# Two forms of an FFN change places, and three weight loads go through DRAM scratch

## What is computed

```python
x = x + attn(layernorm(x))        # time mixing, WKV recurrence, W_o
x = x + ffn(layernorm(x))

def ffn(x):                        # every linear: einsum('bsi,oi->bso', x, w) * s
    h = silu(lin(x, w1)) * lin(x, w2)      # 256 -> 1024
    h = gelu(lin(h, h1))                   # 1024 -> 1024
    h = gelu(lin(h, h2))                   # 1024 -> 1024
    return lin(h, w3)                      # 1024 -> 256
```

## Time and profile before

| | us |
|---|---|
| median of 3 runs | 1565.36 |
| lowest, highest | 1562.19, 1566.46 |
| profiled execution | 1566.22 |
| its span, first to last instruction | 1564.5 |
| PE busy in the span | 1496.0 (96%) |
| DVE busy | 1229.2 (79%) |
| ACT busy | 1091.7 (70%) |

### The profile page before, as it was taken

How to read it: one execution, slowest core, us unless ns; L and a number is a source line. 1 busy time by engine, 2 the same in 40 slices (tenths; PEclk the granted TensorE clock), 3 DMA queues, 4 the chain that set the end, 5 groups by cost and what they waited for, 6 DMA issues and landing times.

```text
span 1564.5 us, 28750 instructions
## 1 busy us (share of the span) xinstructions
PE 1496.0 (96%) x10226; PEld 1329.3 (85%) x10226; DVE 1229.2 (79%) x1595; ACT 1091.7 (70%) x1617; POOL 282.5 (18%) x515
## 2 busy tenths in 40 slices
PE   8489999999999999999999999999999999999997
PEld 5269889898888979889897988989888897988897
DVE  7869696987868788686887968788786878868663
ACT  5848676685867768585776867668585776868564
POOL 0201203112030311204021120311213031120300
PEclk9789999999999999999999999999999999999999
DMA  9957466374655737466474746737465573746654
GB/s 365 350 176 240 124 196 213 105 237 123 205 168 164 239 93 243 108 210 190 131 234 104 232 130 195 214 114 232 127 207 158 161 240 94 242 109 206 181 187 110
DMA packets 95893, 287.78 MB, mean 184 GB/s; under 512 B 9216, under 2 KB 33920, under 8 KB 94848
## 3 DMA queue, kind: packets, MB, share of 16 engines
q1 hardware_dynamic: 87168, 279.11, 54.8%
q0 software_dynamic: 8704, 8.39, 4.5%
HBM read 262.30 MB, written 31.46 MB: 188 GB/s over the span
## 4 chain that ended last, share of the span: by engine, by line
PE 50%; issue 17%; ACT 13%; POOL 10%; DVE 4%; POOLq 1%; ACTq 0%; DVEq 0%
PE acc L540 13%; PE acc L542 12%; PE acc L514 7%; PE acc L515 7%; PE att L466 7%; ACT op_hi L746 3%; ACT blocks L786 3%; POOL fresh L1541 2%; POOL norm L1539 2%; ACT norm L673 2%; POOL newton L1522 1%; PE acc L571 1%; POOL newton L1524 1%; DVE parts L1236 1%; ACT L712 1%
## 5 line engine op out<-in xcount | busy, mean ns | idle before, releaser
L540 PE MATMUL acc<-op_hi,ring 128*128 128x256 f32 x3584 | 865.0, 286 | 1.4 <-DVE parts L1236 1.4
L542 PE MATMUL acc<-op_lo,ring 128*128 128x256 f32 x3584 | 841.5, 278 | 0.0
L540 PEld LDWEIGHTS acc<-op_hi,ring 128*128 128x128 f32 x3584 | 674.1, 188 | 21.0 <-issue 19.9
L542 PEld LDWEIGHTS acc<-op_lo,ring 128*128 128x128 f32 x3584 | 673.3, 188 | 11.9 <-issue 10.8
L1193 DVE TENSOR_TENSOR op_lo<-blocks,op_hi 128x1024 fp32r<-128x1024 f32 (+1 forms) x272 | 343.8, 1283 | 68.0 <-ACT op_hi L746 65.9
L746 ACT ACTIVATE op_hi<-blocks 128x1024 fp32r<-128x1024 f32 (+1 forms) x272 | 297.1, 1104 | 83.8 <-DVE blocks L1188 81.2
L1538 POOL TENSOR_TENSOR v_sb<-mix_v,v_sb 128x1024 f32<-128x1024 f32 (+1 forms) x17 | 39.0, 2293 | 867.7 <-DVE r_sb L1145 867.7
L514 PE MATMUL acc<-x_hi,w_rnd 128*128 128x512 f32 x448 | 180.7, 403 | 5.7 <-issue 5.7
L515 PE MATMUL acc<-x_lo,w_rnd 128*128 128x512 f32 x448 | 178.4, 398 | 0.0
L786 ACT ACTIVATE blocks<-parts,vec 128x256 f32<-128x256 f32 x256 | 109.2, 497 | 60.9 <-DVE parts L1231 52.6
L786 ACT ACTIVATE blocks<-acc,vec 128x256 f32<-128x256 f32 x256 | 100.6, 476 | 66.7 <-PE acc L542 66.7
(11 more groups left out here) (135 smaller groups left out, 1943.9 us busy)
## 6 DMA issues: line engine op xcount, KB each, us to landing
ring<-scratch SPq DMA_DIRECT2D x448, 512.0 KB, 4.2
x_in<-in_x SPq DMA_DIRECT2D x32, 256.0 KB, 4.7
stage<-in_w_ffn SPq DMA_DIRECT2D x4, 2048.0 KB, 22.3
scratch<-stage SPq DMA_DIRECT2D x8, 1024.0 KB, 19.5
out<-x_next SPq DMA_DIRECT2D x32, 256.0 KB, 5.0
out<-mix_v POOLq DMA_DIRECT2D x32, 256.0 KB, 4.5
scratch<-in_w_ffn SPq DMA_DIRECT2D x6, 1024.0 KB, 33.1
w_raw<-in_w_ffn SPq DMA_DIRECT2D x3, 1024.0 KB, 11.6
```

The lines of the kernel that those rows point to most:

```text
L540: pe.matmul(out, act(w), act(op_hi[:, k, c, :]), start=(begins and c == 0 and m % 2 == 0), stop=False, skip_group_check=True)
L542: mm = pe.matmul(out, act(w), act(op_lo[:, k, c, :]), start=False, stop=(c == QC - 1), skip_group_check=True)
```

## The change

PE's `If` takes `flag == 0` with the exact form as its body, and the general form moves to the `Else`. PE's wait for the sums' stores goes (SP keeps its own). `w_rnd` is a tile of its own and `w_raw` a view of it as float32. W1, W2, W3 are copied from the input to a new DRAM tensor `w_plain`, and loaded from there into the tile; the three copies stand ahead of the H loads, the three loads behind them, each after a wait of SP. The three roundings with their flag loads and branches go from ACT, DVE and POOL, as do PE's waits for them. ACT's checks of W1 and W2 move from among the copies of tile 0 to behind the checks of H1's blocks.

```diff
-        w_raw = overlay("w_raw", [P, NW], F32)
         w_rnd = sb("w_rnd", [P, NW], F32R)
+        w_raw = w_rnd[:].bitcast(F32)
...
+        w_plain = nc.dram_tensor("w_plain", [3, P, W12], F32, kind="Internal").ap()
...
-            sp.dma_start(w_raw[:, W1_AT:W1_AT + W12], w_ffn[:, 0:W12]).then_inc(ld_w1, 16)
-            sp.dma_start(w_raw[:, W2_AT:W2_AT + W12], w_ffn[:, W12:2 * W12]).then_inc(ld_w2, 16)
+            for n, a in enumerate((0, W12, 2 * W12 + 2 * HH)):
+                sp.dma_start(w_plain[n], w_ffn[:, a:a + W12]).then_inc(st_w[n], 16)
             for l in range(2):
                 for half in range(2):
                     a = 2 * W12 + l * HH + half * 2 * Q
                     sp.dma_start((stage1, stage2)[l][:, 2 * Q * half:2 * Q * (half + 1)], w_ffn[:, a:a + 2 * Q]).then_inc(ld_h[l][half], 16)
-            sp.dma_start(w_raw[:, W3_AT:W3_AT + W3], w_ffn[:, 2 * W12 + 2 * HH:]).then_inc(ld_w3, 16)
+            for n, (a, loaded) in enumerate(((W1_AT, ld_w1), (W2_AT, ld_w2), (W3_AT, ld_w3))):
+                sp.wait_ge(st_w[n], 16)
+                sp.dma_start(w_raw[:, a:a + W12], w_plain[n]).then_inc(loaded, 16)
...
-                    if exact:
-                        pe.wait_ge(rounded_w1, 1)
-                        pe.wait_ge(rounded_w2, 1)
...
-                    if exact:
-                        pe.wait_ge(rounded_w3, 1)
...
-            for l in range(2):
-                pe.wait_ge(st_sums[l], 16 * 4)
             flag = pe.value_load(general[0:1, 0:1], min_val=0, max_val=1)
-            with pe.If(flag > 0):
+            with pe.If(flag == 0):
+                mlp(exact=True)
+            with pe.Else():
                 mlp(exact=False)
-            with pe.Else():
-                mlp(exact=True)
...
-            check_piece(w_raw[:, W1_AT:W1_AT + W12], (ld_w1, 16))
             for n, s in enumerate(FIRST):
                 copy_kvr(s, 0, range(DC))
-            check_piece(w_raw[:, W2_AT:W2_AT + W12], (ld_w2, 16))
...
             check_blocks(0)
+            check_piece(w_raw[:, W1_AT:W1_AT + W12], (ld_w1, 16))
+            check_piece(w_raw[:, W2_AT:W2_AT + W12], (ld_w2, 16))
             check_sums(0)
...
-            act.wait_ge(flag_set, 1)
-            flag = act.value_load(general[0:1, 0:1], min_val=0, max_val=1)
-            with act.If(flag == 0):
-                rounded(act_copy_, W2_AT, W12).then_inc(rounded_w2, 1)
...
-            dve.wait_ge(flag_set, 1)
-            flag = dve.value_load(general[0:1, 0:1], min_val=0, max_val=1)
-            with dve.If(flag == 0):
-                rounded(dve.tensor_copy, W1_AT, W12).then_inc(rounded_w1, 1)
...
-            pool.wait_ge(flag_set, 1)
-            flag = pool.value_load(general[0:1, 0:1], min_val=0, max_val=1)
-            with pool.If(flag == 0):
-                rounded(pool.tensor_copy, W3_AT, W3).then_inc(rounded_w3, 1)
```

More of the change, by code:

```diff
@@ L284, in build @@
         flag_max = ctx.enter_context(nc.semaphore("flag_max"))
-        rounded_w1, rounded_w2, rounded_w3 = (ctx.enter_context(nc.semaphore(n)) for n in ("rounded_w1", "rounded_w2", "rounded_w3"))
+        st_w = [ctx.enter_context(nc.semaphore(f"st_w{n + 1}")) for n in range(3)]
         W1_AT, W2_AT, W3_AT = 0, W12, 2 * W12
@@ L295, in build @@
         S3_ = [RAW[0][A21_], RAW[1][A21_]]
-        def rounded(copy, a, n):
-            return copy(w_rnd[:, a:a + n], w_raw[:, a:a + n])
         first_chains = Chain(ctx, nc, "first_dve_chain"), Chain(ctx, nc, "first_pool_chain")
@@ L848, in _ @@
             act.wait_ge(setup_pool, 2)
-            def act_copy_(dst, src):
-                return act.activation(dst, src, ACT.Copy)
             checked = [0]
```

## The result

The changed kernel takes 1567.9 us (median of 20 runs, 1565.12 to 1570.53) against 1565.32 for the kernel before beside it (20 runs, 1562.18 to 1568.16): a ratio of 1.0018, with a 95% interval of 1.0012 to 1.0024. It is 2.6 us slower, inside the 0.3% that the prediction called "the same". The profiled run is low among its own: 1565.33 us, with a span of 1563.6.

The account below looks back on a forecast made before the run. It took PE's first FFN matmul (83.82 us) to bound what changes: cheap branch gives 79.3, later checks add 5.5, so 84.8, +1.0 us; median forecast 1566.3 us, range 1562.0 to 1571.0.

Parts of the forecast that it names:

- the gate: Start of PE's first FFN matmul in the first pass, at 83.82 us before, predicted at 84.8.
- The branch: PE's jump to the exact form ahead of the gate: 4.565 us becomes 0.05 by falling through, 4.5 off the gate.
- Binds nothing now: PE's wait for the sums' stores ahead of the flag's load: no effect before, though it would bind at 85.
- the corner: At the gate: flag's load starting before 77.9 without the sums' wait, 78.2 instead of 79.3, at most 1.1 us.
- The end's jump: PE's exact form jumps over the general one at program end: 0.05 to 4.6 us, hidden in 7.7, price 0.
- the end shows: Rival at program end: PE's taken jump costs over 7.7 us and becomes visible, 1567 to 1569 us; chance 0.02.
- The roundings: ACT loses 1.90 us at 74.76, x2 ready 1.8 earlier, but filler and branch hold PE: worth 0.
- The checks: W1's and W2's checks join ACT's row without gaps: 4.2 us, 5.5 later with waiting for the loads.
- The way through DRAM: Three extra weight copies, 9.3 us more DMA: W1 back at 43.3, W2 at 45.7, last sums near 85.
- The rival of copies slower than 340 GB/s: Copies into w_plain run slower and shift all behind: at 4 us a piece gate 87.6, 1569.1 us; chance 0.07.
- x for the next tile: First pass: x_in, queued behind the sums, lands about 87.3 to 88.5; 88.9 still free; price 0.
- from there to ln1 are 6.6 us: First pass: from DVE starting on x_in to ACT's ln1, through POOL's last step, takes 6.6 us.

Follow-up runs that it names:

- swap alone: Kernel before with one edit: PE's If takes flag == 0 with the exact form as its body, general form in the Else; 1560.86 us, ratio 0.9974.
- without the wait: Kernel before with PE's two forms exchanged and PE's waits for the sums' stores removed; 1562.15 us, ratio 0.9981.
- with x early: Kernel before with forms exchanged, PE's wait for the sums' stores gone, next tile's x loaded ahead of those stores; 1561.47 us, ratio 0.9975.
- swap and checks: Kernel before with forms exchanged and ACT's checks of W1 and W2 moved behind those of H1's blocks, weights straight from the input; 1565.8 us, ratio 1.0000.
- x early: Changed kernel with next tile's x loaded ahead of the sums' stores, DVE waiting for these before its first product; 1564.36 us, 0.9997 against the kernel before.

## Why the prediction came out as it did

**Result.** Forecast +1.0 us (1566.3, range 1562.0 to 1571.0) and "the same" at 0.81; it came to +2.6, the same by that bound, and slower beyond the measurement's error. The structure held: a gain and a loss of nearly one size. Several terms were mis-sized, and that the sum came this near is partly luck: the errors went both ways. By the traces the gate is 0.75 us later (83.4 for 82.7, means of three), the second pass 0.9, and the end adds 0.6.

**The branch.** Predicted 4.5 off the gate, measured 4.0 alone. The mechanism was right (0.095 us where it falls through), the term was too large by some 0.7, as one trace gave 4.565 and three give a mean of 3.87. The gate of that first trace was late for this reason, and because its wait for the sums ended later. The branch's length may go with the traffic: 3.37, 3.67 and 3.94 us where DMA was under half busy beside it, 4.35 and 4.57 (and once 6.29) where it was full. No run varied the traffic alone.

**The sums' wait.** "Binds nothing now" was wrong. In the earlier trace rows the filler starts at 76.12 and the flag's load at 77.9; in the swap alone they are 76.26 and 76.4, in the changed kernel 81.89 and 81.9. The load starts with the filler, not behind it, so the wait was what held it to 77.8, by 1.6 us in that trace and by about 0.5 in the two others (filler at 76.62 and 76.74, load at 77.2 and 77.3). The last store of a sum lands at 77.8, 77.1 and 77.1 in these traces, which is when the wait ends. Together with the roundings (below) this is why the corner that the prediction kept for its range came true. The predicted gate was 84.8, with the corner 83.7, and the traces have 83.26, 83.29 and 83.75.

**The end's jump.** Priced at 0, with 7.7 us of cover, and this was wrong by about 0.6. From DVE's last product to POOL's last store are 1.72 to 2.15 us in the six traces whose PE has no jump there (mean 1.88), and 2.21 to 2.71 in the eight with it (mean 2.46). In each of the eight the store starts 0.6 us after the jump's end: 1553.1 + 3.86 = 1556.96 and 1557.57 in the changed kernel, 1552.0 and 1552.66 in the swap alone. The step that failed compared PE's jump with the gap to POOL's drain, as if nothing else in that gap could be held up. Whether the store waits for something of PE's or the two fetch code beside each other the traces don't say: the profile names no releaser. The mild end of the rival "the end shows" was right in kind.

**The roundings.** Priced at 0, and the rows speak against it. From x1's copy to the gate are 11.2 us in the four traces with cheap branch and roundings (swap alone, without the wait, with x early, swap and checks: 11.17 to 11.18), and 10.6 in the three of the changed kernel (10.56 to 10.59): x2 is ready 1.5 us earlier there (DVE's last rest ends 9.5 us after x1's copy instead of 11.0), and it was x2 that held the gate. The step that failed is "with the branch cheap this gives nothing", since the sum put the flag's load behind the filler and so hid x2. But that first matmul then runs beside the filler's end (1.10 us for 0.79), and at the second one only 0.3 us are left. No run took the roundings alone.

**The checks.** A delay of 5.5 us was predicted for x1's copy (72.9), and it stands at 72.70. The two checks give 4.2, as predicted. W1 and W2 landed at 43.2 and 45.6, where the prediction had 43.3 and 45.7, so its way through DMA was right. They held ACT for only some 0.2 us, not 1.3, because the row itself began 1.0 later, a term that wasn't in the sum. The two don't add: W2's landing fixes when its check can start. With x early the row began at 36.71 and had to wait more, and x1's copy still came at 72.82. PE's first products, at L466 before and L463 after, in the two kernels, each beside the clock of 16 to 18 us (columns as above):

```profile
16.14 4.30 PE L466 MATMUL acc<-mix_k,wm 128*128 128x256 f32 x16
...
16.00:18.00 2.00, 2.00 (x7) 1.54 (x6) 1.96 (x5) 0.16 (x2) 0.00 (x0) 0.62 1.02 438
```

```profile
16.11 5.36 PE L463 MATMUL acc<-mix_k,wm 128*128 128x256 f32 x16
...
16.00:18.00 2.00, 2.00 (x6) 1.51 (x5) 1.96 (x5) 0.00 (x0) 0.00 (x0) 0.50 1.08 389
```

The granted clock came back from the lower of its two levels, 1.2 GHz, later. The same 16 matmuls took 4.3 to 4.8 us in the three traces of before and 5.2 to 5.7 in those of the changed kernel. Over all fourteen traces it goes mostly with the place of the checks: 4.3 to 4.8 in five of the six with the checks in their old place (the sixth, the swap without the wait, has 5.66), 5.1 to 5.7 in seven of the eight with the checks moved (the eighth, x early, has 4.64). Whether moving the checks makes the clock come back later, or it is scatter of about a microsecond, isn't shown.

**The way through DRAM.** It was to be hidden but for late W. It was, up to the gate, thanks to the wait that went. The rival of copies slower than 340 GB/s didn't come: W1 was in time. The last sums land at 85.8, 85.5 and 85.4, near 85 as predicted.

**x for the next tile.** Here the price of 0 was wrong. The landing was forecast at 87.3 to 88.5, and DVE takes x up at 88.71 (88.39 and 88.20 in the two further traces). That is nearly right, for another reason than "queued behind the sums": the load is asked for 4.1 us later, behind ACT's rounding of x2, and with the traffic left out x is as late (88.16 with swap and checks). The step that failed is "from there to ln1 are 6.6 us". It takes 8.1, since POOL's steps run beside DVE's: a step of 0.20 us took 1.26 beside DVE's TENSOR_TENSOR of 1.22. In the first trace of before these steps lay beside gaps of DVE or its products with an input in PSUM; in the two further ones the way takes 8.5 and 7.9, so the 6.6 was a price from one trace. Then ACT waits 1.75 us for ln1, while PE is idle for only 0.13 us ahead of its transposes at 98.98. The wait tells further on: in the seven traces where ACT waits over 1 us ahead of ln1 (the changed kernel three times, the swap with and without the wait, swap and checks, the second of before), the second pass starts 82.3 to 82.5 us behind ln1's start and in the seven others 83.0 to 83.8 (four of the fourteen first passes end in a stretch of the lower clock, for which 1.25 us are taken off). So in the seven the second pass seems to hang on x and ln1, and not on the gate. The Trainium skill, "SBUF — State Buffer", section "SBUF: two separate sides", says that DVE's operations with two SBUF inputs and GpSimd's lock each other out of a shared pair of ports for the whole instruction. The rows agree: the POOL step ended with DVE's, and DVE's product with one input in PSUM at 94.00 left POOL's steps at 0.20.

**What stays open.** The changed kernel is 2 us over swap and checks alone (1.0013 [1.0004, 1.0022] and 1.0018 [1.0012, 1.0024] against 1.0000 [0.9991, 1.0009]), so what remains of the change, the way through DRAM with the roundings and the wait gone, costs about that (2.0 and 2.8 us by the ratios; each of the three has an interval of 0.9 to 1.4 us either way). The traces don't show it: the second pass begins at 179.28, 178.97 and 178.80 in the changed kernel, at 178.93 with swap and checks, and at 179.02, 178.31 and 177.00 in the kernel before. So changed less before is 0.9 at the second pass, and 0.6 more at the end: 1.5 of the 2.0 to 2.6 that were measured, which the interval allows. Swap and checks should by the same rows have cost as much, 0.8 + 0.6, and measured 0.1, with 1.4 either way. That x early takes 3.1 us back points at x_in. But x is as late with swap and checks (ln1 at 96.58, and at 96.84, 96.53 and 96.33 in the changed kernel), which is 2 us faster; so a late x that both have can't be the difference between them. One thing that sets them apart could count in runs that weren't traced: where the row of checks begins early, the changed kernel can't use it, as W2 lands at 45.6 all the same. And the profiled runs of the changed kernel are all below its median (1565.33, 1565.22, 1566.82), and what the slower runs do wasn't profiled. The mean granted clock of the runs is not lower (0.984 over the 20 runs, 0.983 for the kernel before beside the experiments), so it isn't that.

**The best version** is the swap alone: 1560.86 us, 0.9974, faster than both kernels, with one edit of order. The two variants of it (without the wait, and with x early too) can't be told from it.

## What to carry to other kernels

Put the form that runs where the branch falls through: the far jump cost 3.4 to 6.3 us each time at the gate, the fall-through 0.1, and a jump moved to the end of PE's program only 0.6 of its 4. Before moving work out of a wait, see whether its new place is an engine's row without gaps; there each moved check cost its full 2.1 us. Extra DMA traffic was paid here at a wait that stood on its end, 5.0 us, and hardly at all at the gate where no such wait was, so look for these first. When something comes late, look at when it was asked for before blaming the queue; and take the size of a term that comes once per program, such as a branch, from more than one trace.

## What the runs showed of the hardware

- The far branch, taken once, took 3.37, 3.67, 3.94, 4.35 and 4.57 us at the gate, 6.29 once (DMA was full beside it, but also beside the 4.35 and 4.57), 3.7 to 4.2 at the end, where POOL's last store came 0.6 later with it. PE's fifteen jumps back over a pass took 0.08 to 0.25 each in the same programs.
- A POOL step of 0.20 us took up to 1.26 beside a DVE operation with two SBUF inputs.
- Within a program PE falls to the lower clock for 3.4 us at a pass boundary, where it has waited a little (0.62 and 1.12 us ahead of the fall at 734.3 in the first trace), 372 or 464 us apart, at boundaries that differ from trace to trace. Two traces of the kernel before, the same stretch (columns as above):

```profile
735.00:738.00 3.00, 3.00 (x15) 2.86 (x14) 0.64 (x2) 0.00 (x0) 0.00 (x0) 0.55 0.00 0
```

```profile
735.00:738.00 3.00, 3.00 (x17) 2.54 (x16) 2.17 (x8) 0.69 (x1) 0.91 (x1) 1.00 0.00 0
```

The first is the profiled run of the tables, at 0.55, the second a further one, at 1.00. Each such boundary costs some 1.5 us (a pair of passes takes 93.8 + 92.8 instead of 2 x 92.56), and the traces have two to four of them in the loop. The three traces of before have three, four and four of them, those of the changed kernel two, two and three, 2 us less on average, which can be why their spans are alike (1564.5, 1564.2, 1563.8 and 1563.6, 1563.5, 1565.1) although the medians are not.

- At the gate the clock is at its lower level too, in every trace, until 1.7 to 5.4 us after the first FFN matmul. No term of the prediction covers this.
